# Seven channel tiles of the last FFN block convolved by TensorE, with second products, row maxima and scaling laid out anew in the slot before it

## The chip, the core and the metric

The kernel runs on one core of a Trainium2 chip: TensorE (PE), VectorE (DVE), ScalarE (ACT), GpSimd (POOL), and SyncE (SP), which issues the DMAs. The metric is the device time of one execution in microseconds, lower is better.

## The reference, cut to what matters

The input x is 4 batches x 2048 rows x 512. A cross attention adds to it first; then comes the FFN, of which the change touches the last block of rows:

```python
h = bit_linear(x, w1)                     # act_quant: each row scaled by 127 / its largest |value|, rounded
h = depthwise_conv1d(h.transpose(0, 2, 1), conv_w, conv_b)   # 2048 channels, 3 taps along the rows, padding 1
h = jax.nn.silu(h.transpose(0, 2, 1))
return bit_linear(h, w2)                  # the same quantisation, now over the row's 2048 channels
```

bit_linear uses weights rounded to -1, 0 and 1. Its row maximum makes the second product wait until all 2048 channels of a row are there. The outputs of this layer are x plus attention, plus the FFN of the layer norm of that.

## The kernel before, in words

The 8192 rows go in 16 blocks of 512 (NB = 16), the FFN's 2048 channels in 16 tiles of 128 (CT = 16). Each engine runs its own list of instructions in the order in which the code is written, and semaphores tie the lists together. The work is staged in slots. In slot s the kernel projects the queries of block s + 1, does the attention of block s, the first product, convolution and silu of block s - 1, and the second product of block s - 2. Slot NB - 1 = 15 is the last with attention; slot NB = 16 has only the FFN middle of the last block and the second product of the one before; slot 17 is the last block's second product, whose result is stored as the program's end.

The FFN middle of one channel tile c goes through five steps. TensorE forms the first product (`mm1`, L864) in one of two PSUM banks. `dequant` on VectorE (L1591) scales it into g, a ring of four buffers, so that tile c waits until tile c - 4 is convolved. `neighbours` on ScalarE (L1164) copies the two edge columns, `tap0` (L1262) forms the first tap, `taps` on VectorE (L1666) adds the middle one. The third tap is GpSimd's (L642 multiplies, L644 adds) for the tiles in `TAP.pool`, otherwise VectorE's (L1670). Then ScalarE does the silu (L1267). In slot 16 GpSimd has ten tiles of the third tap, VectorE six.

After the middle, VectorE takes the maxima over all channels (L1675, in the last block L1684), TensorE turns them (`turn_pm`, L1020), VectorE forms the scales (`scales2`), TensorE spreads them over the partitions (`spread_scales`, L1026), and ScalarE copies them to r2. Then h is multiplied by r2 (`scaled`: L654 on GpSimd, L1756 on VectorE), ScalarE rounds it to hqb (`rounded`, L1164), and `mm2` (L1042, in slot 17 L1144) is the second product. `result` (L1790) adds it to the rows. Slot 16 also computes again the outputs of the 12 rows at the ends of the blocks (the functions whose names begin with fix), on a few partitions or columns.

In slot 15 the attention's output is turned (`turn_o`, L946) and projected (`project_out`, L956); `residual` (L1736), `centre` (L1324), `square` (L1329) and `quantise` lead to the rounded rows (L1439), which TensorE turns (`turn_xq`, L1003) for the first product of slot 16.

## Time and profile before

| | before |
|---|---|
| median of 3 runs | 1532.26 us (1530.31 to 1534.05) |
| the profiled execution's own time | 1529.84 us |
| its span, first to last instruction | 1528.0 us |
| busy in the span | PE 95%, DVE 85%, ACT 77%, POOL 68% |
| mean granted TensorE clock | 0.977 |

The shares are means over 18 slots. The change touches only what runs after about 1394 us; there PE is busy 67% of the stretch from 1437 to 1487 us, and VectorE 86%. All the times below are in us from the first instruction. The granted clock is 1.00 for 2.4 GHz and 0.50 for 1.2 GHz.

### The profile page before, as it was taken

The numbers are of one execution on the slowest core, as the hardware profiler recorded it, in microseconds if no ns is written. First come the engines' busy times: TensorE is split into PE (matmuls) and PEld (weight loads), VectorE is DVE, ScalarE is ACT, GpSimd is POOL, SyncE is SP. The second block draws the span as 40 slices with busy tenths as digits, with TensorE's granted clock in tenths as the row PEclk, the third lists the DMA queues.
The fourth block names the chain that finished last, engine by engine and source line by source line (L and its number), as shares of the span: only waits on it lengthen the run. The fifth ranks groups of instructions, "written<-read, shape, count | busy, mean of one in ns | idle before, by whom it ended". The sixth has DMA issues, their size and how long they took to land.

```text
span 1528.0 us, 24767 instructions
## 1 busy us (share of the span) xinstructions
PE 1446.3 (95%) x9060; PEld 886.2 (58%) x9060; DVE 1298.4 (85%) x2014; ACT 1184.1 (77%) x2176; POOL 1035.2 (68%) x838
## 2 busy tenths in 40 slices
PE   9998988999999999999999999999999999998866
PEld 6474745657575656656575656656574756555322
DVE  7787796897979898898979898898989898978796
ACT  3567788979687888879687878889687878887652
POOL 4011567868676968869676869778776869777552
PEclk9998999999999999999999999999999999998987
DMA  8551002030211203031202103031202101020000
GB/s 260 147 189 42 29 8 70 8 102 18 68 42 27 79 8 98 8 102 22 78 29 50 55 9 96 8 102 29 87 12 63 43 23 54 8 71 1 31 29 28
DMA packets 80343, 85.20 MB, mean 56 GB/s; under 512 B 29983, under 2 KB 55839, under 8 KB 79709
## 3 DMA queue, kind: packets, MB, share of 16 engines
q1 hardware_dynamic: 80221, 83.62, 18.9%
q8 instruction: 71, 1.16, 0.3%
q14 instruction: 51, 0.42, 0.1%
HBM read 38.74 MB, written 19.42 MB: 38 GB/s over the span
## 4 chain that ended last, share of the span: by engine, by line
PE 67%; DVE 19%; ACT 9%; issue 3%; POOL 2%; DMA 0%; SPq 0%; DVEq 0%; ACTq 0%
PE ps L858 13%; PE ps L683 12%; DVE negm L1750 11%; PE ps L956 10%; PE ps L864 10%; PE ps L1042 8%; ACT hqb L1164 4%; ACT pexp L1243 3%; PE ps L827 3%; DVE h L1666 2%; PE ps L946 2%; PE ps L924 1%; PE ps L1026 1%; POOL h L644 1%; PE ps L1012 1%
## 5 line engine op out<-in xcount | busy, mean ns | idle before, releaser
L644 POOL TENSOR_TENSOR h<-h,gall 128x512 f32<-128x512 f32 x235 | 347.9, 1480 | 18.4
L654 POOL TENSOR_TENSOR h<-h,r 128x512 f32<-128x512 f32 x240 | 306.7, 1324 | 58.9 <-ACT r L1164 58.9
L642 POOL TENSOR_TENSOR gall<-gall,cw 128x512 f32<-128x512 f32 x235 | 257.5, 1096 | 111.0 <-DVE h L1666 111.0
L1666 DVE SCALAR_TENSOR_TENSOR h<-gall,cw,h 128x512 f32<-128x512 f32 x256 | 261.9, 1026 | 49.5 <-ACT h L1262 49.3
L858 PEld LDWEIGHTS ps<-va,pexp 128*128 128x128 f32 x2048 | 259.5, 192 | 29.0 <-issue 10.9
L1591 DVE SCALAR_TENSOR_TENSOR gall<-ps,bias,srow 128x512 f32<-128x512 f32 x256 | 191.3, 747 | 86.7 <-POOL h L644 57.7
L864 PE MATMUL ps<-xqT,w1T 128*128 128x512 f16 x1024 | 258.0, 382 | 7.1 <-DVE gall L1591 7.1
L858 PE MATMUL ps<-va,pexp 128*128 128x33 f32 x2048 | 257.7, 270 | 0.0
L1042 PE MATMUL ps<-w2T,hqb 128*128 128x512 fp8e4 x960 | 240.2, 379 | 0.0
L1262 ACT ACTIVATE h<-gall,cb,cw 128x512 f32<-128x512 f32 x256 | 222.2, 868 | 8.5
L1243 ACT ACTIVATE pexp<-ps 128x512 f32<-128x512 f32 x320 | 179.5, 588 | 54.5 <-PE ps L827 27.7
L1164 ACT ACTIVATE hqb<-h 128x512 f16<-128x512 f32 x276 | 173.9, 683 | 39.4 <-PE ps L1042 18.1
L1750 DVE TENSOR_REDUCE negm<-ps 128x4 f16<-128x616 f32 x256 | 185.7, 792 | 19.9 <-PE ps L975 14.8
L683 PE MATMUL ps<-hl,WqT 128*128 128x512 f16 x768 | 170.8, 379 | 2.7 <-DVE hl L1708 2.6
L1267 ACT ACTIVATE h<-h 128x512 f32<-128x512 f32 x256 | 155.4, 684 | 12.3 <-POOL h L644 11.7
L956 PE MATMUL ps<-WoT,pexp 128*128 128x512 f16 x512 | 156.0, 381 | 2.5 <-DVE xn L1729 2.5
L864 PEld LDWEIGHTS ps<-xqT,w1T 128*128 128x128 fp8e4 x1024 | 102.1, 112 | 85.9 <-DVE gall L1591 11.7
L1042 PEld LDWEIGHTS ps<-w2T,hqb 128*128 128x128 f16 x960 | 92.3, 98 | 80.9 <-issue 1.8
L658 POOL TENSOR_TENSOR nw<-nw,mhalf 128x4 f32<-128x4 f32 x16 | 16.3, 1017 | 175.7 <-DVE nw L1760 175.7
L683 PEld LDWEIGHTS ps<-hl,WqT 128*128 128x128 f16 x768 | 74.2, 98 | 91.5 <-issue 8.0
L975 PE MATMUL ps<-kB,hl 128*128 128x308 f16 x512 | 116.1, 305 | 10.9 <-DVE negm L1750 8.5
L1324 ACT ACTIVATE xn<-xr,sum 128x512 f32<-128x512 f32 x64 | 44.1, 717 | 80.9 <-DVE xr L1736 75.6
(222 smaller groups left out, 2312.0 us busy)
## 6 DMA issues: line engine op xcount, KB each, us to landing
qs<-hl SPq DMA_DIRECT2D x192, 128.0 KB, 2.4
xr<-in_x SPq DMA_DIRECT2D x16, 1024.0 KB, 5.4
out<-xr SPq DMA_DIRECT2D x64, 256.0 KB
h<-in_L_ffn_w SPq DMA_DIRECT2D x8, 1024.0 KB, 5.2
srow<-in_L_xattn_bo SPq DMA_DIRECT2D x15, 256.0 KB, 3.1
kst<-kh_scratch SPq DMA_DIRECT2D x32, 38.5 KB
xr<-in_ctx SPq DMA_DIRECT2D x1, 1024.0 KB
h<-in_L_xattn_Wk SPq DMA_DIRECT2D x1, 1024.0 KB, 8.0
```

The costliest lines, as they stand in the source:

```text
L642: gp.tensor_tensor(right, right, cw[:, c, 2:3].to_broadcast([P, TB]), ALU.mult).then_inc(c2m_ok, 1)
L644: gp.tensor_tensor(hc(c), hc(c), right, ALU.add).then_inc(c2p_ok, 1)
L654: gp.tensor_tensor(hc(c), hc(c), r2[:], ALU.mult).then_inc(u_ok, 1)
L683: r = mm(bank, a, b_, start=i == 0, stop=i == n - 1, **kw)
L858: r = mm(o, pr[:, t * P:(t + 1) * P], rhs, start=j == 0 and t % 2 == 0, stop=j == J, skip_group_check=True)
L864: r = mm(F[(c + 1) % 2], w1T[:, k, c * P:(c + 1) * P], xqT[:, k, :], start=k == 0, stop=k == KT - 1)
L956: r = mm(bank, part(k)[:, i * P:(i + 1) * P], WoT[:, a, k, :], start=k == 0 and n == 0, stop=k == KT - 1 and n == 2)
L1042: r = mm(bank, hq(c)[:, i * P:(i + 1) * P], w2T[:, c, :], start=False, stop=c == CT - 1, skip_group_check=late_results(s))
L1164: return nc.scalar.activation(o, i, ACT.Copy, **kw)
L1243: nc.scalar.activation(pexp[:, i % 3, :], A[i % 2], ACT.Exp, scale=1.0 / QS).then_inc(e_ok, 1)
L1666: ve.scalar_tensor_tensor(out=hc(c), in0=g[:, c % 4, 1:TB + 1], scalar=cw[:, c, 1:2], in1=hc(c), op0=ALU.mult, op1=ALU.add).then_inc(c1_ok, 1)
L1750: ve.tensor_reduce(negm[:, i, k * J:(k + 1) * J].rearrange("p (b e) -> p b e", b=2), banks, AX.X, ALU.max, negate=True).then_inc(mx_ok, 1)
```

## The change

In slot 16 the odd channel tiles 1 to 13 (`CONV`) leave ScalarE's tap0, VectorE's taps and the third tap. TensorE convolves each by three f32 products of 512 columns with diagonal matrices of the tap weights, in PSUM banks A[2] and A[3], and ScalarE's silu reads PSUM and adds the bias. GpSimd keeps the third tap of eight tiles, VectorE that of tile 15. ScalarE makes the 21 diagonals of 128x128 in slot 15, in the space of the queries.

In slot 15 pieces of the second product (`mm2`) go ahead of and behind `turn_o`. VectorE's first two residuals go between the two maxima. All 16 tiles are scaled by GpSimd: ten in slot 15, six within slot 16, two behind each of the taps of tiles 0, 2 and 4. ScalarE rounds none of them before slot 16 and spreads the 16 roundings over its ten first steps by `NEXT`.

In slot 16 the second product of the block before moves to the end of the slot, with its four results; tile 0 to 7's maxima come ahead of the taps of tile 14. `fix_mm2` moves ahead of slot 17's products, and the small fix products use other banks.

```diff
@@ tables
+        CONV = (1, 3, 5, 7, 9, 11, 13)
+        def mid(s, c):
+            return at(s, CT, c + 1 - CT) - (sum(n <= c for n in CONV) if s == NB else 0)
-        TAP = Share((0, 1, 2, 3, 4, 5, 6, 8, 9, 10, 11, 12, 13, 14, 15), last=(0, 2, 3, 5, 6, 8, 9, 11, 12, 14))
-        SCALE = Share(tuple(range(CT)), last_but_one=(0, 1, 3, 4, 6, 7, 9, 10, 12, 14), last=(1, 4, 7, 10, 12, 14))
+        TAP = Share((0, 1, 2, 3, 4, 5, 6, 8, 9, 10, 11, 12, 13, 14, 15), elsewhere=CONV, last=(0, 2, 4, 6, 8, 10, 12, 14))
+        SCALE = Share(tuple(range(CT)), last_but_one=tuple(range(CT)), last=(1, 4, 7, 10, 12, 14))
-            return 8 if s < NB - 1 else 4
+            return 8 if s < NB - 1 else 0
+        NEXT = (0, 0, 2, 3, 4, 5, 7, 9, 11, 13, 16)
@@ GpSimd
+                    if s == NB and c in (0, 2, 4):
+                        scaled(range(10 + c, 12 + c))
...
-                    scaled(SCALE.pool(s))
+                    scaled(range(10) if s == NB - 1 else SCALE.pool(s))
@@ TensorE
+                def conv(c):
+                    n = CONV.index(c)
+                    if n == 0:
+                        pe.wait_ge(dg_ok, 3 * len(CONV))
+                    if n >= 2:
+                        pe.wait_ge(si_ok, at(s, CT, CONV[n - 2] + 1 - CT))
+                    pe.wait_ge(g_ok, at(s, CT, c + 1 - CT))
+                    for k in (1, 2, 0):
+                        if k == 0:
+                            pe.wait_ge(nb_ok, at(s, CT, c + 1 - CT))
+                        r = mm(conv_bank(c), dg[:, n, k, :], g[:, c % 4, k:TB + k], start=k == 1, stop=k == 0)
+                    r.then_inc(cv_ok, 1)
...
+                    if c >= 2 and on_pe(s, c - 2):
+                        conv(c - 2)
...
-                    if s == NB and c in (8, 10, 12, 14):
-                        mm2((c - 8) // 2)
+                    if s == NB and c in (14, 15):
+                        mm2(0, range(CT // 2 * (c % 2), CT // 2 * (c % 2 + 1)))
...
+                        if s == NB - 1:
+                            mm2(0, range(0, 11))
                         turn_o()
+                        if s == NB - 1:
+                            mm2(0, range(11, CT))
+                            mm2(1, range(0, 4))
...
                 if s == NB:
+                    mm2(1)
                     fix_turn_pm()
+                    mm2(2, range(0, 8))
                     fix_scales()
+                    mm2(2, range(8, CT))
+                    mm2(3, range(0, 8))
                 if do_f:
                     turn_pm()
-                if do_a and do_m:
+                if s == NB:
+                    mm2(3, range(8, CT))
@@ ScalarE
+                def diagonal(n, k):
+                    nc.scalar.activation(dg[:, n, k, :], identf[:], ACT.Copy, scale=cw[:, CONV[n], k:k + 1]).then_inc(dg_ok, 1)
+                def silu_conv(c):
+                    act.wait_ge(cv_ok, CONV.index(c) + 1)
+                    nc.scalar.activation(hc(c), conv_bank(c), ACT.Silu, bias=cb[:, c:c + 1]).then_inc(si_ok, 1)
@@ VectorE
-                    if s == NB and c in (10, 12, 14, 16):
-                        result((c - 10) // 2)
-                    if s == NB and c == 14:
+                    if s == NB and c == 13:
                         fix_conv()
+                    if s == NB and c == 16:
+                        absmax_last(0, 4, pm)
+                        fix_absmax()
...
-                    for c in SCALE.dve(s)[:3]:
-                        scaled(c)
                     result(2)
-                    for c in SCALE.dve(s)[3:]:
-                        scaled(c)
                     result(3)
                 if s == NB:
                     fix_scaled()
+                    for i in range(1, TT):
+                        result(i)
                     for c in SCALE.dve(s):
                         scaled(c)
```

The first place is GpSimd's list from the end of slot 15 on. L654 is the scaling (it writes h with the factors r2), L642 and L644 are the third tap, L637 is the inverse root of the fix rows. Before:

```order
L654 TENSOR_TENSOR h<-h,r 128x512 [waits r2c,ln2]
L654 TENSOR_TENSOR h<-h,r 128x512 x9
L642 TENSOR_TENSOR gall<-gall,cw 128x512 [waits c1_ok]
L644 TENSOR_TENSOR h<-h,gall 128x512 [waits c2m_ok]
L642 TENSOR_TENSOR gall<-gall,cw 128x512 [waits c1_ok]
L644 TENSOR_TENSOR h<-h,gall 128x512 [waits c2m_ok]
L642 TENSOR_TENSOR gall<-gall,cw 128x512 [waits c1_ok]
L644 TENSOR_TENSOR h<-h,gall 128x512 [waits c2m_ok]
L637 TENSOR_TENSOR xn<-xn,mhalf 36x1 [waits fx_dve]
L642 TENSOR_TENSOR gall<-gall,cw 128x512 [waits c1_ok]
```

And now, where L660, L673, L675 and L668 are the same four:

```order
L660 TENSOR_TENSOR h<-h,r 128x512 [waits r2c,ln2]
L660 TENSOR_TENSOR h<-h,r 128x512 x9
L673 TENSOR_TENSOR gall<-gall,cw 128x512 [waits c1_ok]
L675 TENSOR_TENSOR h<-h,gall 128x512 [waits c2m_ok]
L660 TENSOR_TENSOR h<-h,r 128x512 x2
L673 TENSOR_TENSOR gall<-gall,cw 128x512 [waits c1_ok]
L675 TENSOR_TENSOR h<-h,gall 128x512 [waits c2m_ok]
L660 TENSOR_TENSOR h<-h,r 128x512 x2
L668 TENSOR_TENSOR xn<-xn,mhalf 36x1 [waits fx_dve]
L673 TENSOR_TENSOR gall<-gall,cw 128x512 [waits c1_ok]
L675 TENSOR_TENSOR h<-h,gall 128x512 [waits c2m_ok]
L660 TENSOR_TENSOR h<-h,r 128x512 x2
```

Two scalings stand behind each of the first three taps, so the tap of tile 2 and the inverse root come later in the list.

The second place is ScalarE's list in the second half of slot 15, from the centring of the attention's rows (L1324) to the rounded rows (L1439). Before:

```order
L1324 ACTIVATE xn<-xr,sum 128x512 [waits x2_ok] x2
L1324 ACTIVATE xn<-xr,sum 128x512 [waits op_ok,x2_ok]
L1324 ACTIVATE xn<-xr,sum 128x512 [waits x2_ok]
L1329 ACTIVATE osb,sq<-xn 128x512 [waits zx_ok] x4
L1164 ACTIVATE r<-ps 128x512 [waits r2_ok]
L1439 ACTIVATE osb<-xr,qb,qm 128x512 [waits ln2]
L1439 ACTIVATE osb<-xr,qb,qm 128x512 x3
L1164 ACTIVATE xqT<-ps 128x512 [waits xqt_ok] x4
```

And now (L1326 makes diagonals, L1400 centres, L1405 squares, L1524 rounds):

```order
L1326 ACTIVATE qs<-identf,cw 128x128 x6
L1400 ACTIVATE xn<-xr,sum 128x512 [waits x2_ok] x2
L1326 ACTIVATE qs<-identf,cw 128x128 x6
L1400 ACTIVATE xn<-xr,sum 128x512 [waits op_ok,x2_ok]
L1326 ACTIVATE qs<-identf,cw 128x128 x3
L1400 ACTIVATE xn<-xr,sum 128x512 [waits x2_ok]
L1405 ACTIVATE osb,sq<-xn 128x512 [waits zx_ok] x4
L1326 ACTIVATE qs<-identf,cw 128x128 x6
L1224 ACTIVATE r<-ps 128x512 [waits r2_ok]
L1524 ACTIVATE osb<-xr,qb,qm 128x512 [waits ln2]
L1524 ACTIVATE osb<-xr,qb,qm 128x512 x3
L1224 ACTIVATE xqT<-ps 128x512 [waits xqt_ok] x4
```

Nine diagonals stand between the second and the fourth centring, six between the squares and the copy of the factors.

The third place is TensorE's list in slot 16 from the first product of tile 8 (L864) on. Before:

```order
L864 MATMUL ps<-xqT,w1T 128x512 [waits g_ok]
L864 MATMUL ps<-xqT,w1T 128x512 x3
L864 MATMUL ps<-xqT,w1T 128x512 [waits g_ok]
L864 MATMUL ps<-xqT,w1T 128x512 x3
L1040 MATMUL ps<-csum,negh 128x512 [waits hq_ok]
L1042 MATMUL ps<-w2T,hqb 128x512 x16
L864 MATMUL ps<-xqT,w1T 128x512 [waits g_ok]
L864 MATMUL ps<-xqT,w1T 128x512 x3
L887 MATMUL ps<-identh,osb 128x36 [waits fx_act]
L887 MATMUL ps<-identh,osb 128x36 x3
L889 MATMUL ps<-identf,xn 128x36
L864 MATMUL ps<-xqT,w1T 128x512 [waits g_ok]
L864 MATMUL ps<-xqT,w1T 128x512 x3
```

And now (L893 is the first product, L907 the convolution by diagonals, L930 and L932 are fix_turn, L938 is fix_mm1):

```order
L893 MATMUL ps<-xqT,w1T 128x512 [waits g_ok]
L893 MATMUL ps<-xqT,w1T 128x512 x3
L893 MATMUL ps<-xqT,w1T 128x512 [waits g_ok]
L893 MATMUL ps<-xqT,w1T 128x512 x3
L907 MATMUL ps<-gall,qs 128x512 [waits g_ok,si_ok]
L907 MATMUL ps<-gall,qs 128x512
L907 MATMUL ps<-gall,qs 128x512 [waits nb_ok]
L930 MATMUL ps<-identh,osb 128x36 [waits fx_act]
L930 MATMUL ps<-identh,osb 128x36 x3
L932 MATMUL ps<-identf,xn 128x36
L893 MATMUL ps<-xqT,w1T 128x512 [waits g_ok]
```

The second products (L1042) are gone from here, and three f32 products stand behind the first product of each odd tile.

## Rows read from the trace of the kernel before

**Rows 1.** Windows by stage: span of the stretch, busy us of each engine, PE clock

```profile
1437.07:1486.73 49.66, 33.45 (x195) 13.51 (x194) 42.87 (x61) 33.78 (x66) 30.62 (x25) 0.89 0.08 29
1486.73:1498.25 11.52, 0.97 (x3) 0.58 (x3) 11.30 (x12) 1.22 (x2) 1.23 (x1) 0.50 0.00 0
```

**Rows 2.** Timeline, slot 15: start, length, engine, line, idle before and its releaser

```profile
1415.04 1.95 ACT L1324 ACTIVATE xn<-xr,sum 128x512 f32<-128x512 f32 x3 [5.82 <-DVE xr L1736]
...
1417.46 0.72 ACT L1324 ACTIVATE xn<-xr,sum 128x512 f32<-128x512 f32 x1 [0.48 <-DVE xr L1736]
...
1420.67 0.17 DVE L1760 TENSOR_SCALAR nw<-sq 128x4 f32<-128x4 f32 x1
...
1423.57 0.17 DVE L1783 TENSOR_SCALAR qb<-qb 128x4 f32<-128x4 f32 x1
...
1425.68 0.60 ACT L1164 ACTIVATE r<-ps 128x512 f32<-128x512 f32 x1 [5.05 <-PE ps L1026]
...
1429.60 0.90 PEld L1003 LDWEIGHTS ps<-identh,osb 128*128 128x128 f16 x16 [0.58 <-ACT osb L1439]
```

**Rows 3.** Groups by shape, ScalarE, whole run: count, busy us, mean ns

```profile
L1164 ACT ACTIVATE gall<-gall 128x2 f32<-128x2 f32 x256 | 51.7, 202 | 6.6 <-DVE gall L1591 6.2
L1164 ACT ACTIVATE xn<-xn 128x192 f16<-128x192 f32 x1 | 0.4, 363 | 11.9 <-DVE xn L1657 11.9
```

**Rows 4.** Timeline, from slot 15 to 16

```profile
1436.40 4.63 ACT L1164 ACTIVATE hqb<-h 128x512 f16<-128x512 f32 x8 [3.58 <-PE ps L1042]
...
1437.07 1.40 DVE L1591 SCALAR_TENSOR_TENSOR gall<-ps,bias,srow 128x512 f32<-128x512 f32 x2
...
1442.87 1.04 POOL L642 TENSOR_TENSOR gall<-gall,cw 128x512 f32<-128x512 f32 x1 [1.19 <-DVE h L1666]
```

**Rows 5.** GpSimd's groups: three in 1436 to 1487 us, the scaling in the whole run

```profile
L644 POOL TENSOR_TENSOR h<-h,gall 128x512 f32<-128x512 f32 x10 | 15.6, 1558 | 0.8
L642 POOL TENSOR_TENSOR gall<-gall,cw 128x512 f32<-128x512 f32 x10 | 10.8, 1082 | 18.3 <-DVE h L1666 18.3
L637 POOL TENSOR_TENSOR xn<-xn,mhalf 36x1 f32<-36x1 f32 x1 | 1.0, 1001 | 0.0
...
L654 POOL TENSOR_TENSOR h<-h,r 128x512 f32<-128x512 f32 x240 | 306.7, 1324 | 58.9 <-ACT r L1164 58.9
```

**Rows 6.** Timeline, TensorE: f32 products at both clocks, first products at both

```profile
1430.51 1.11 PE L1012 MATMUL ps<-identf,qm 128*128 128x128 f32 x8
...
1444.49 1.80 PE L864 MATMUL ps<-xqT,w1T 128*128 128x512 f16 x4 [3.70 <-DVE gall L1591]
...
1451.61 1.04 PE L864 MATMUL ps<-xqT,w1T 128*128 128x512 f16 x4 [0.67 <-DVE gall L1591]
...
1500.89 2.08 PE L1026 MATMUL ps<-identf,qm 128*128 128x128 f32 x8 [1.52 <-DVE qm L1704]
```

**Rows 7.** VectorE, slot 16: two groups of 1436 to 1487 us, then its timeline

```profile
L1666 DVE SCALAR_TENSOR_TENSOR h<-gall,cw,h 128x512 f32<-128x512 f32 x16 | 14.2, 893 | 2.3 <-ACT h L1262 2.3
...
L1670 DVE SCALAR_TENSOR_TENSOR h<-gall,cw,h 128x512 f32<-128x512 f32 x6 | 8.8, 1473 | 0.2
...
1454.46 0.15 DVE L1604 TENSOR_TENSOR xn<-xn 36x1 f32<-36x1 f32 x1 [0.45 <-POOL xn L637]
...
1456.68 0.14 DVE L1621 TENSOR_SCALAR xn<-xn 36x1 f32<-36x1 f32 x1
...
1474.20 0.81 DVE L1628 TENSOR_TENSOR xn<-ps,bias 128x288 f32<-128x288 f32 x2
...
1478.33 0.36 DVE L1638 TENSOR_TENSOR xn<-xn,cb 128x192 f32<-128x192 f32 x1
```

**Rows 8.** Timeline, from the end of slot 16 to the last products

```profile
1503.68 10.32 POOL L654 TENSOR_TENSOR h<-h,r 128x512 f32<-128x512 f32 x6 [15.72 <-ACT r L1164]
...
1509.22 13.99 PE L1144 MATMUL ps<-w2T,hqb 128*128 128x512 fp8e4 x64
...
1514.59 4.02 ACT L1164 ACTIVATE hqb<-h 128x512 f16<-128x512 f32 x7 [1.03 <-DVE h L1756]
```

More of the change, by code:

```diff
@@ L374, in dve @@
             def dve(self, s):
-                return tuple(c for c in range(CT) if c not in self.pool(s))
+                return tuple(c for c in range(CT) if c not in self.pool(s) and not (s == NB and c in self.elsewhere))
             def done(self, s, c):
@@ L630, in slot, with scaled @@
                 do_q, do_a, do_f, do_m = stages(s)
+                def scaled(tiles):
+                    for c in tiles:
+                        gp.tensor_tensor(hc(c), hc(c), r2[:], ALU.mult).then_inc(u_ok, 1)
                 for c in range(CT):
@@ L1372, in slot @@
                     if do_m and s != NB + 1:
-                        for k in range(early(s - 1) + 2 * c, min(early(s - 1) + 2 * c + 2, CT)):
+                        for k in late_roundings(s, c):
                             rounded_late(k)
@@ L1838, in slot @@
                         norm1()
-                    if do_f and c >= 2:
+                    if do_f and c >= 2 and not on_pe(s, c - 2):
                         taps(c - 2)
@@ L1878, in slot @@
                     centred_max(1)
+                if s == NB:
+                    result(0)
                 if do_f:
```

94 lines of the change are left out of this document (65 added, 29 removed).

## The prediction

> **What bounds the kernel now.** I read the windows by stage first, then the chain that ended last, then the timeline from 1379 us on, with the two instruction lists beside it. Up to slot 15 both lists are the same, so the first 1394 us can't change. Behind them no engine is full. From 1437 to 1487 us, the FFN middle of the last block, TensorE is busy 33 of 50 us, GpSimd 31, ScalarE 34, VectorE 43 [rows 1]. There each of VectorE's instructions waits for another engine's turn, or shares its time with GpSimd's: the middle tap has a mean of 0.89 us, the third tap 1.47 [rows 7]. Then come 11.5 us of maxima on VectorE, with TensorE idle at clock 0.50 [rows 1], and at the end the last scalings, roundings and 64 products, which run to 1523.2 us [rows 8]. So what counts is how early each of four handovers comes: the rounded rows in slot 15, the first dequantised tile, the last tile's maxima, the first scaling by r2.
>
> **The change, step by step.**
>
> *Slot 15, to the turned rows.* TensorE's pieces of the second product go where it waits anyway, and the row factors no longer stand behind two whole second products: the copy of r2 waited 5.05 us for TensorE [rows 2]. What is late next is ScalarE. A diagonal has 128 columns, between the 2 columns at 0.20 us and the 192 at 0.36 [rows 3]; by the line between them 0.30 us. Six of the 21 go where ScalarE waited 5.82 us for the first residual [rows 2]. The two residuals between the maxima leave VectorE's sum alone, so the second residual still ends at about 1415. From there: centring 0.65, six diagonals 1.8, centring 0.65, three diagonals 0.9, centring 0.7, to 1419.7 instead of 1418.2 [rows 2]. The squares end 1.5 us later, at 1422.1 instead of 1420.67, and the quantising scalars, which take 3.1 us to 1423.7 [rows 2], end at 1425.2. The last six diagonals and the copy of r2 run meanwhile. The rounded rows took 3.3 us from 1426.3 on, so TensorE can turn them at 1428.5, not 1429.6 [rows 2]: 1.1 us won.
>
> *Into slot 16.* Before, eight products of the last second product ahead of the first product, eight more behind it, and six scalings on VectorE put the first dequantisation at 1437.07, and eight roundings of 4.63 us kept ScalarE from tile 0 until 1441 [rows 4]. Now five products of 0.22 us [rows 8] follow the turned rows (1.1 us) and the spread row (1.0), the first product ends at 1432.5, and the dequantisation starts at 1432.6; ScalarE has two roundings and is at tile 0 by 1433.4. VectorE's tap of tile 0 is there at 1436. But GpSimd isn't: its ten scalings begin at 1425.2 with the scalars and take 10 x 1.32 [rows 5], to 1438.4. It was 1442.87 [rows 4]: 4.5 us won of some 7.5.
>
> *GpSimd, then the fix rows.* GpSimd is now the late one. It goes on with the tap of tile 0 (1.08 + 1.56 [rows 5], 2.7 with the handover), two scalings, the tap of tile 2, two scalings and the inverse root of the fix rows (1.0): 5.4 + 5.3 + 1.0 puts the root at 1450.2. It ended at 1454.4 [rows 7], so this wait moves forward too, though its list has become longer by four scalings. The fix scalars stand ahead of the dequantisation of tile 7, and behind that are queued TensorE's first product of tile 9 and all behind it. They take 2.4 us [rows 7], the dequantisation 0.7 [rows 4]: 1453.3. The fix rows' loads from memory start behind the fourth result and so some 4.7 us earlier; they stay ahead of this.
>
> *TensorE in slot 16.* A convolution is three f32 products of 512 columns, and the trace has no such product. It has f32 products of 128 columns: four of them (recorded as eight) take 1.11 us at full clock with the drain of the last, 0.24 each from start to start, and 2.08 at half clock [rows 6]. Four times the columns give 0.86 to 0.96; the lower end is what the columns alone make of it, and I take it: 2.6 us for a tile, 18 us for seven. The most, at half clock throughout, is 5.2 a tile. From 1453.3 TensorE has first product 9, convolution 7, the fix turn, first products 10 and 11, convolution 9, the 64 small fix products and first product 12: 4 x 0.87 + 2 x 2.6 + 0.6 + 1.8 = 11.1 us. Before it TensorE has waited some 5 us; after waiting 3.7 us its clock was down and a first product took 1.80 instead of 1.04 [rows 6], so I add 1.8. First product 12 ends at 1466.2.
>
> The Trainium skill (Perfetto Trace Analysis, Engine Utilization) rates f32 in its low-high form at half of TensorE's peak; by it a 512-column product would be 0.43 us, an estimate, two convolutions of this list 2.6 us shorter and the forecast 2.6 us lower. FP8 and Floating Point Precision (TensorE Precision Notes) gives true f32 four passes, an estimate of 0.85 us. The row of 0.24 us for 128 columns sides with four passes.
>
> *VectorE to the last maximum.* From there VectorE is the path: dequantisation and tap 1.6, the small convolution of the fix rows 4.5 (1474.20 to 1478.7 [rows 7]), tiles 13, 14, 15 and the tap of 12 another 3.0, the maxima 11.5 [rows 1], and among them the taps of 14 and 15, 0.9 + 0.9 + 1.5 [rows 7]. That is 23.9 us, to 1490.1, against 1498.25: 8.1 us won. The seven tiles that VectorE and ScalarE no longer tap shorten lists that now wait for GpSimd and TensorE; in themselves they pay nothing more.
>
> *To the first scaling.* Two things are given back. TensorE has 17 products of 0.22 behind the fix scales, which come from VectorE 2.9 us ahead of its last maximum (one reduction of half length and a merge): 1487.2 + 0.4 + 3.7 = 1491.3, with 0.5 for a clock that may be down, 1491.8 for the turn. The turn and the spread are 1.5 us shorter at full clock [rows 6]; eight products of 1.75 lie between them over the 1.4 of scalars; and three results of 0.75 stand ahead of VectorE's first scaling. GpSimd starts at 1495.8, VectorE at 1496.5, instead of 1503.68 [rows 8]: 7.2 to 7.9 won.
>
> *The end.* The scalings and roundings keep their shape: 10.9 us from the first scaling to the last seven roundings [rows 8], so these start at about 1507.3. Their first is ready 0.6 later, and seven tiles of four products at 0.22 need 6.1: 1514.0. TensorE alone: spread at 1495.2, the fix product of 17 x 0.22 (now at full clock) and four preparing ones to 1499.8, then 13.99 [rows 8] to 1513.8. Both ends meet. It was 1523.2 with the drain of the last product, some 1522.6 without it. I take 8.5 us off. The profiled execution took 1529.84, so 1521.3; the median lies 2.4 us above it, which gives 1523.8. A measurement tells about 0.2% (3 us) from no change.
>
> **The rivals.**
>
> *GpSimd's price is the contended one.* I charge 1.32 us a scaling. When VectorE scaled at the same time it was 10.32 for six, 1.72 [rows 8]. Now VectorE mostly reads PSUM beside it in slot 15, but in slot 16 it taps. With 1.72 for the 14 scalings ahead of the root, 5.6 us are lost and 2.9 of the gain remain: 1529.4. For it speaks that GpSimd is now at the head of the chain; against it that the mean over 240 is 1.32 with VectorE busy beside it [rows 5]. GPSIMD Engine Reference (Key points) of the Trainium skill says that GpSimd contends with VectorE's instructions with two SBUF inputs; by this rule the four scalings in slot 16 pay and the ten in slot 15 mostly don't. 14 in 100.
>
> *Slower: the f32 products run at half clock.* All 35 us or so of first products and convolutions in slot 16 would double where the clock is 0.50. From 1453.3 to first product 15 TensorE has 17.5 us of work; at half clock throughout that is 15.7 us more than I allow, VectorE's list behind it has 1 us of slack, and the end moves by 14.5 to 6 us slower than before: 1538. It decides from about half of this stretch at the low clock on. The clock was 0.89 in this stretch with a less busy TensorE [rows 1], which speaks against it; what speaks for it is that each convolution waits for ScalarE and a silu. 8 in 100.
>
> *The gain is given back.* The late parts of slot 16 are a list of handovers I have priced at 0.05 to 0.1 us each. If the fix products, the scales and the second products block each other in TensorE's order by some 3 us twice, the outcome is within 3 us of before: 1531. 8 in 100.
>
> *More is won.* If TensorE's clock doesn't fall (1.8 and 0.5), the diagonals take 0.25, and the third taps lose their contention, as they have only one partner (0.3 x 4), 12 us are won: 1520 or a little lower. 8 in 100.
>
> My forecast has the rest, 62 in 100; its own range is a gain of 4.5 to 12 us.
>
> **How the numbers follow.** Faster: the forecast, more won, and two thirds of the contended case, 0.79. Same: the other third and most of the gain given back, 0.12. Slower: half clock and the rest, 0.09. The range runs from 1517.5, beyond the case of more won, to 1530, which takes in the contended case; half clock and part of the gain given back are left out.
>
> **What would show it.** Right: GpSimd without a gap from 1425 to the inverse root near 1450; three f32 products of 2.6 us in a tile's place; a TensorE gap of 5 us ahead of first product 9; maxima done near 1490; the last products near 1514. Wrong: ScalarE's diagonals much above 0.30, scalings of 1.5 and more, convolutions of 4 to 5 us, or results that hold VectorE's scalings beyond 1498.

## The result, and the profile after

The changed kernel takes 1521.57 us, the median of 4 runs (1519.37 to 1523.01), the kernel before 1532.49 (4 runs, 1530.31 to 1534.05): a ratio of 0.9934, with an interval of 0.9914 to 0.9953. 1523.8 was predicted, with a range of 1517.5 to 1530. The profiled execution took 1519.37 us with a span of 1517.6 and a mean granted clock of 0.988, against 1528.0 and 0.977. It was the shortest of the four.

Not all of the 10.4 us between the two spans comes from the change. The first of the view's rows below is GpSimd's inverse root in the first slot, the second the same root in slot 14, both far ahead of anything that was changed. In these rows the columns are start, length, engine, line, what is written from what, shapes, the number of instructions, and in brackets the idle time before it with what ended that. Before:

```profile
146.46 1.02 POOL L658 TENSOR_TENSOR nw<-nw,mhalf 128x4 f32<-128x4 f32 x1 [28.48 <-DVE nw L1760]
...
1339.33 1.02 POOL L658 TENSOR_TENSOR nw<-nw,mhalf 128x4 f32<-128x4 f32 x1 [9.82 <-DVE nw L1760]
```

After:

```profile
144.21 1.02 POOL L687 TENSOR_TENSOR nw<-nw,mhalf 128x4 f32<-128x4 f32 x1 [28.30 <-DVE nw L1847]
...
1337.15 1.02 POOL L687 TENSOR_TENSOR nw<-nw,mhalf 128x4 f32<-128x4 f32 x1 [9.79 <-DVE nw L1847]
```

2.25 us are there at the first root and 2.18 at slot 14's: the two executions differ in how long the preparation took, and in next to nothing from there to slot 14. Over all the kernels below, the first root lies between 144.21 and 148.56 us and slot 14's between 1337.15 and 1344.03, though the instructions ahead of them are the same. So I count from the root of slot 14 on; from there to the end it is 188.67 us before and 180.45 after, and the change itself has won **8.2 us**. The interval of the ratio is 7.2 to 13.2 us of gain, and 8.2 lies in it. In the table every time is counted so. It needs no more than subtraction: the row's start (or end) less the start of slot 14's root.

| from slot 14's root on, us | before | after | won | forecast |
|---|---|---|---|---|
| slot 16's first dequantisation | 97.74 | 93.19 | 4.6 | 4.5 |
| GpSimd's first tap | 103.54 | 98.74 | 4.8 | 4.5 |
| fix rows' inverse root, end | 115.10 | 109.96 | 5.1 | 4.2 |
| last maximum, end | 158.87 | 152.27 | 6.6 | 8.1 |
| VectorE's first scaling by r2 | 164.31 | 157.83 | 6.5 | 7.2 |
| last 64 products, start | 169.89 | 161.64 | 8.3 | |
| last instruction | 188.67 | 180.45 | 8.2 | 8.5 |

GpSimd from slot 15 on, in the changed kernel's timeline, where [rows 4, 5] stood before:

```profile
1422.89 13.03 POOL L660 TENSOR_TENSOR h<-h,r 128x512 f32<-128x512 f32 x10 [1.88 <-DVE qb L1870]
1435.89 1.04 POOL L673 TENSOR_TENSOR gall<-gall,cw 128x512 f32<-128x512 f32 x1
1437.01 1.30 POOL L675 TENSOR_TENSOR h<-h,gall 128x512 f32<-128x512 f32 x1
1438.26 3.01 POOL L660 TENSOR_TENSOR h<-h,r 128x512 f32<-128x512 f32 x2
...
1446.56 0.55 POOL L668 TENSOR_TENSOR xn<-xn,mhalf 36x1 f32<-36x1 f32 x1
...
1462.11 1.04 POOL L673 TENSOR_TENSOR gall<-gall,cw 128x512 f32<-128x512 f32 x1 [5.33 <-DVE h L1753]
```

It runs without a gap from 1422.89 to the inverse root at 1446.56, as forecast, at 1.30 us a scaling in slot 15 and 1.50 for the four ahead of the root in slot 16. From then on it waits, 5.33 us ahead of one tap: it was the late one only up to the root.

VectorE at the fix scalars, the tiles behind them, and the last maxima [rows 7 before]:

```profile
1447.15 0.99 DVE L1691 TENSOR_TENSOR xn<-xn 36x1 f32<-36x1 f32 x1 [1.70 <-POOL xn L668]
1448.17 0.15 DVE L1693 SCALAR_TENSOR_TENSOR xn<-xn 36x1 f32<-36x1 f32 x1
1448.36 1.14 DVE L1696 SCALAR_TENSOR_TENSOR xn<-xn 36x1 f32<-36x1 f32 x1
1449.54 1.48 DVE L1699 TENSOR_SCALAR osb<-osb,xn 36x512 f32<-36x512 f32 x1
...
1452.22 1.41 DVE L1678 SCALAR_TENSOR_TENSOR gall<-ps,bias,srow 128x512 f32<-128x512 f32 x2
...
1460.62 0.75 DVE L1678 SCALAR_TENSOR_TENSOR gall<-ps,bias,srow 128x512 f32<-128x512 f32 x1 [4.85 <-PE ps L893]
...
1488.73 0.69 DVE L1776 TENSOR_TENSOR pm<-pm,pexp 128x512 f32<-128x512 f32 x1
...
1491.40 0.69 DVE L1781 TENSOR_REDUCE qm<-ps 128x4 f32<-128x512 f32 x1 [1.32 <-PE ps L1063]
1494.98 12.54 DVE L1843 TENSOR_TENSOR h<-h,r 128x512 f32<-128x512 f32 x10
```

From the root to the next dequantisation it is 5.1 us (1447.15 to 1452.22). L1691 works on 36 numbers and takes 0.99; the row of this shape took 0.15 before [rows 7]. Beside these rows, GpSimd's of the same time are to be laid, still of the changed kernel:

```profile
1447.09 1.03 POOL L673 TENSOR_TENSOR gall<-gall,cw 128x512 f32<-128x512 f32 x1
1448.20 1.29 POOL L675 TENSOR_TENSOR h<-h,gall 128x512 f32<-128x512 f32 x1
1449.44 2.71 POOL L660 TENSOR_TENSOR h<-h,r 128x512 f32<-128x512 f32 x2
```

VectorE's L1691 ends at 1448.14, GpSimd's L673 at 1448.12. L1693 starts at 1448.17, in the 0.08 us between two of GpSimd's instructions, and takes 0.15. L1696 ends at 1449.50, GpSimd's L675 at 1449.49. L1699 ends at 1451.02, GpSimd's first scaling of this pair at 1450.73. The kernel before shows the same instructions with GpSimd waiting beside them for 3.83 us, and L1699's pass over 36x512 (there L1612) takes 0.54, not 1.48:

```profile
1455.02 0.54 DVE L1612 TENSOR_SCALAR osb<-osb,xn 36x512 f32<-36x512 f32 x1
...
1458.26 1.04 POOL L642 TENSOR_TENSOR gall<-gall,cw 128x512 f32<-128x512 f32 x1 [3.83 <-DVE h L1666]
```

TensorE in the same stretch, with the three f32 products as L907, and the end [rows 6, 8 before]:

```profile
1432.88 2.74 PE L907 MATMUL ps<-gall,qs 128*128 128x512 f32 x6
...
1453.03 1.89 PE L893 MATMUL ps<-xqT,w1T 128*128 128x512 f16 x4 [7.50 <-DVE gall L1678]
1454.70 4.41 PE L907 MATMUL ps<-gall,qs 128*128 128x512 f32 x6
...
1486.56 0.39 PE L948 MATMUL ps<-identf,xn 12*128 12x12 f32 x2 [1.74 <-DVE xn L1740]
1486.88 1.90 PE L1087 MATMUL ps<-w2T,hqb 128*128 128x512 fp8e4 x8
...
1490.76 0.60 PE L1063 MATMUL ps<-identf,pm 128*128 128x128 f32 x4
...
1498.79 14.18 PE L1206 MATMUL ps<-w2T,hqb 128*128 128x512 fp8e4 x64
```

A convolution (three products, recorded as six) takes 2.74 us at full clock, counted to the end of its last product, which still runs while the next instruction has started. The one behind the wait of 7.50 us takes 4.41. Its granted clock stands in the windows (length, busy us of PE, PEld, DVE, ACT and POOL, clock):

```profile
1430.34:1482.67 52.33, 44.31 (x208) 19.02 (x206) 35.56 (x47) 27.94 (x58) 33.21 (x28) 0.90 0.03 8
1482.67:1489.42 6.75, 5.01 (x22) 2.01 (x23) 6.58 (x11) 1.23 (x2) 1.23 (x1) 1.00 0.00 0
...
1449.00:1450.00 1.00, 0.00 (x0) 0.00 (x0) 0.96 (x2) 0.00 (x0) 1.00 (x2) 0.50 0.00 0
...
1456.00:1458.00 2.00, 2.00 (x3) 0.67 (x2) 0.00 (x0) 1.97 (x4) 0.79 (x1) 0.50 0.00 0
1458.00:1459.00 1.00, 1.00 (x3) 0.19 (x1) 0.00 (x0) 0.04 (x1) 0.00 (x0) 0.97 0.00 0
```

The clock fell during the wait, and was back at 1458. Where the maxima ran at 0.50 before [rows 1], TensorE now has second products beside them and stays at 1.00. Over the FFN middle, TensorE is busy 44 of 52 us and VectorE only 36. From 1453.03 on TensorE's list is what VectorE waits for (4.85 us once, in the rows above): until 1484.8 TensorE itself waits only once, for 0.47 us.

### The profile page after: what moved, and what is told of

The parts are those of the page before. It is cut to its first block and busy times, and to the rows that moved or that the text cites. A ratio compares the mean times of both kernels' runs of the same rounds, so it can differ in the third digit from the quotient of the medians.

```text
span 1517.6 us, 24856 instructions
## 1 busy us (share of the span) xinstructions
PE 1456.6 (96%) x9102; PEld 890.7 (59%) x9102; DVE 1270.8 (84%) x1996; ACT 1185.8 (78%) x2190; POOL 1035.4 (68%) x840
## 5 line engine op out<-in xcount | busy, mean ns | idle before, releaser
L675 POOL TENSOR_TENSOR h<-h,gall 128x512 f32<-128x512 f32 x233 | 344.9, 1480 | 18.2
L660 POOL TENSOR_TENSOR h<-h,r 128x512 f32<-128x512 f32 x246 | 313.1, 1318 | 50.9 <-ACT r L1224 49.0
L673 POOL TENSOR_TENSOR gall<-gall,cw 128x512 f32<-128x512 f32 x233 | 255.3, 1096 | 109.8 <-DVE h L1753 109.8
L1753 DVE SCALAR_TENSOR_TENSOR h<-gall,cw,h 128x512 f32<-128x512 f32 x249 | 253.4, 1020 | 46.9 <-ACT h L1322 46.7
L887 PEld LDWEIGHTS ps<-va,pexp 128*128 128x128 f32 x2048 | 259.5, 192 | 29.0 <-issue 10.9
L893 PE MATMUL ps<-xqT,w1T 128*128 128x512 f16 x1024 | 256.1, 380 | 8.1 <-DVE gall L1678 8.0
L1322 ACT ACTIVATE h<-gall,cb,cw 128x512 f32<-128x512 f32 x249 | 216.4, 869 | 8.3
L1341 ACT ACTIVATE h<-h 128x512 f32<-128x512 f32 x249 | 151.0, 684 | 13.8 <-POOL h L675 13.4
L893 PEld LDWEIGHTS ps<-xqT,w1T 128*128 128x128 fp8e4 x1024 | 101.8, 111 | 86.1 <-DVE gall L1678 11.8
L1400 ACT ACTIVATE xn<-xr,sum 128x512 f32<-128x512 f32 x64 | 44.3, 717 | 77.8 <-DVE xr L1823 71.4
```

What stands on the lines that cost most here:

```text
L660: gp.tensor_tensor(hc(c), hc(c), r2[:], ALU.mult).then_inc(u_ok, 1)
L673: gp.tensor_tensor(right, right, cw[:, c, 2:3].to_broadcast([P, TB]), ALU.mult).then_inc(c2m_ok, 1)
L675: gp.tensor_tensor(hc(c), hc(c), right, ALU.add).then_inc(c2p_ok, 1)
L887: r = mm(o, pr[:, t * P:(t + 1) * P], rhs, start=j == 0 and t % 2 == 0, stop=j == J, skip_group_check=True)
L893: r = mm(F[(c + 1) % 2], w1T[:, k, c * P:(c + 1) * P], xqT[:, k, :], start=k == 0, stop=k == KT - 1)
L1322: nc.scalar.activation(hc(c), g[:, c % 4, 0:TB], ACT.Identity, bias=cb[:, c:c + 1], scale=cw[:, c, 0:1]).then_inc(c0_ok, 1)
```

## The experiments

Each was timed beside the kernel before on its chip. Repeated runs of one kernel lie 1 to 7 us apart, and in the profiles much of that lies ahead of slot 14's root, so the reading goes by the profile from that root on. "End" is that time: 188.67 before, 180.45 after. The first four go out from the changed kernel.

Each kernel has one profile, so two things are to be kept in mind. Where kernels have the same lists up to a point, their times from the root on agree closely: slot 16's first dequantisation stands at 91.74 to 91.78 us in e4, e6, e9 and e10. But TensorE's clock can fall in one execution ahead of the turn of the maxima and not in another, and this alone moves the end by 1.6 us (below, under e6). Differences under 2 us at the end are therefore read at the last maximum too. The timed ratios are too coarse for them: e4's is no better than the changed kernel's, and e5's no better than e2's.

| | timed ratio | end | root | last maximum | first VectorE scaling |
|---|---|---|---|---|---|
| before | | 188.67 | 115.10 | 158.87 | 164.31 |
| after | 0.9934 | 180.45 | 109.96 | 152.27 | 157.83 |
| e1, no convolution on TensorE | 0.9990 (0.9980 to 0.9999) | 188.12 | 112.54 | 157.13 | 165.49 |
| e2, slot 15 of before | 0.9935 (0.9918 to 0.9952) | 178.63 | 110.44 | 150.44 | 156.00 |
| e3, root early | 0.9919 (0.9899 to 0.9938) | 177.28 | 101.67 | 147.47 | 154.62 |
| e4, diagonals early | 0.9941 (0.9923 to 0.9959) | 179.40 | 108.54 | 151.19 | 156.75 |
| e5, e2 with root early | 0.9941 (0.9918 to 0.9963) | 178.02 | 106.45 | 148.25 | 155.40 |
| e6, e3 and e4 | 0.9910 (0.9891 to 0.9930) | 174.23 | 100.21 | 146.02 | 151.57 |
| e7, e6, VectorE scales too | 0.9917 (0.9893 to 0.9941) | 175.25 | 103.18 | 145.46 | 152.61 |
| e8, e5, eight products moved up | 0.9948 (0.9932 to 0.9964) | 181.44 | 106.45 | 150.38 | 158.86 |
| e9, e6, fix rows a step earlier | 0.9907 (0.9890 to 0.9923) | 174.17 | 100.24 | 144.39 | 151.54 |
| e10, e6, six tiles on TensorE | 0.9924 (0.9911 to 0.9938) | 177.58 | 100.25 | 147.07 | 154.98 |

**e1: without the convolution.** The seven tiles get their taps from ScalarE, VectorE and GpSimd again, and there are no diagonals; all else is as in the changed kernel.

```diff
-        CONV = (1, 3, 5, 7, 9, 11, 13)
-        TAP = Share(..., elsewhere=CONV, last=(0, 2, 4, 6, 8, 10, 12, 14))
+        CONV = ()
+        TAP = Share(..., elsewhere=CONV, last=(0, 2, 3, 5, 6, 8, 9, 11, 12, 14))
```

> The changed kernel without its convolution on TensorE: CONV is empty, all tiles go through the three taps, GpSimd has the third tap of the ten tiles of before. Everything else stays. The change as a whole won 10.9 us in the medians and 8.3 us in the two traces from slot 14's inverse root to the end. Theory: the convolution is what makes the room, since GpSimd is at the head of slot 16 and has six scalings more; without it VectorE has 42 us of work in slot 16 again, with waits some 46, and the maxima end 6 to 9 us later than in the changed kernel, so that 0 to 3 us of the gain over before are left. Rival: the gain comes from slot 15 and from taking the second products out of slot 16's middle; then the time stays within 2 us of the changed kernel.

The end is at 188.12, 0.55 us ahead of before. So 7.7 of the 8.2 us need the convolution on TensorE; everything else that was moved is worth 0.55 without it. The maxima come 1.7 us earlier than before, but the first scaling 1.2 us later: VectorE then waits 4.11 us for the turn, behind TensorE's second products, sixteen of which take 3.59 and 2.57 us. Their clock had fallen in an earlier wait of 4.50 us: it stands at 1.00 from 1483 to 1485 us of this trace and at 0.50 from 1486 to 1498. At the last maximum the convolution is worth 4.9 us (157.13 against 152.27). The reverse, the convolution without any of the rearrangement, was not run; e2 comes nearest to it.

**e2: slot 15 of before.** The pieces of the second product, the residuals, the scalings (six on VectorE) and the early roundings stand where they stood before, and GpSimd has no scalings in slot 16. The diagonals stay where the change put them, nine of them between the centrings.

```diff
-        SCALE = Share(tuple(range(CT)), last_but_one=tuple(range(CT)), last=(1, 4, 7, 10, 12, 14))
+        SCALE = Share(tuple(range(CT)), last_but_one=(0, 1, 3, 4, 6, 7, 9, 10, 12, 14), last=(1, 4, 7, 10, 12, 14))
-                        if s == NB - 1:
-                            mm2(0, range(0, 11))
...
-                        if s == NB - 1:
-                            mm2(0, range(11, CT))
-                            mm2(1, range(0, 4))
```

> The changed kernel with slot 15 as before (second products, residuals, six scalings on VectorE, four roundings at its end, no scalings in slot 16), the diagonals stay. Theory, GpSimd at the head: its last scaling in slot 15 then ends at some 1441 us instead of 1436, but two taps later it is without the four scalings, so the inverse root of the fix rows comes within 1.5 us of where it does in the changed kernel, and the end with it: 0 to 2.5 us slower than the changed kernel. Rival, each handover is handed on: slot 16 starts 4.5 to 6 us later (first dequantisation some 7 us later) and the end is 4.5 to 6 us later.

It is 1.8 us faster, and I had expected it no faster. Slot 16 begins 4.9 us later, but the root ends only 0.5 later, since GpSimd has four scalings fewer ahead of it, and TensorE arrives later at the same wait. In e2's timeline it is 2.00 us long, and the clock stays up: the convolution behind it takes 2.74 us, not 4.41. From slot 14's root, TensorE goes on at 116.5 us here and at 115.9 in the changed kernel; the new slot 15 is 0.6 ahead there and then loses the 2.5 us of the low clock.

```profile
1455.09 1.04 PE L891 MATMUL ps<-xqT,w1T 128*128 128x512 f16 x4 [2.00 <-DVE gall L1669]
1455.96 2.74 PE L905 MATMUL ps<-gall,qs 128*128 128x512 f32 x6
```

**e3: the inverse root early.** It goes right behind the tap of tile 0, ahead of the four scalings and a tap, and the fix scalars one tile earlier.

```diff
-                    if s == NB and c == 4:
-                        pool.wait_ge(fx_dve, 3)
-                        gp.tensor_tensor(fnw[:, 1:2], fnw[:, 0:1], mhalf[0:N3, 0:1], ALU.pow).then_inc(fx_pw, 1)
+                    # the same three lines at c == 0, behind the tap of tile 0
-                    if s == NB and c == 7:
+                    if s == NB and c == 6:
                         fix_quantise()
```

> The changed kernel with GpSimd's inverse root of the fix rows right behind the tap of tile 0, ahead of all scalings of slot 16, and the fix rows' scalars on VectorE ahead of tile 6 instead of tile 7, where VectorE waited 2.9 us. Theory: the wait for this root held TensorE 7.5 us and let its clock fall; without it the dequantisation of tile 7 comes at 1446 to 1447 us of the changed kernel's trace instead of 1452.2, the convolution of tile 7 takes 2.7 instead of 4.4, and the end is 3 to 7 us earlier. Rival, GpSimd's load itself is the bound: the root was only one item, the taps of tiles 6 to 14 come at GpSimd's own pace and the end is at most 1.5 us earlier.

3.2 us faster: the wait at the root was what slot 16 lost. The maxima gain 4.8, the first scaling only 3.2. The missing 1.6 us are TensorE's second products ahead of the turn (L1063), most of them at half the clock in this execution:

```profile
1484.53 0.39 PE L948 MATMUL ps<-identf,xn 12*128 12x12 f32 x2 [1.75 <-DVE xn L1740]
1484.85 3.17 PE L1087 MATMUL ps<-w2T,hqb 128*128 128x512 fp8e4 x8
...
1488.49 2.00 PE L1087 MATMUL ps<-w2T,hqb 128*128 128x512 fp8e4 x8
1490.33 0.60 PE L1063 MATMUL ps<-identf,pm 128*128 128x128 f32 x4
```

The eight products behind L948, which took 1.90 us after a wait of 1.74 in the changed kernel, take 3.17 here after one of 1.75. The clock fell after TensorE had taken up work again: it is 1.00 from 1484.6 to 1485.2 and 0.50 from 1485.4 to 1488.6. VectorE's fix scalars still take 4.6 us here, at another place against GpSimd's list.

**e4: the diagonals early.** Nine diagonals go ahead of the second centring, where ScalarE waits, instead of between centrings.

```diff
+                    if s == NB - 1:
+                        diagonals(2, 5)
                     centre(1)
-                    if s == NB - 1:
-                        diagonals(2, 4)
                     centre(2)
-                    if s == NB - 1:
-                        diagonals(4, 5)
```

> The changed kernel with the nine diagonals that stood around the third centring moved ahead of the second centring, where ScalarE waited 3.3 us. Theory: they were on the path by 1.4 us, so squares, scalars and GpSimd's first scaling come 1.2 to 1.6 us earlier, and as GpSimd is at the head, the end too. Rival: VectorE's residuals or the second products set this handover, and the first scaling moves by under 0.4 us.

GpSimd's first scaling comes 1.4 us earlier, the end 1.05. The prediction's 1.5 us for the diagonals in the chain of centrings is measured with that.

**e5 and e6: the four corners.** e6 is e3 and e4 together. e5 is e2 with the early root, and with all fifteen diagonals that are due before the squares ahead of the first centring. In slot 15 of before these diagonals cost nothing: GpSimd's first scaling starts at 87.13 us in e2 and at 87.08 in e5.

> Slot 15 as before, and with it the two edits that helped singly: the root of the fix rows behind the tap of tile 0, and all 15 diagonals of the middle of slot 15 ahead of the first centring, where ScalarE waits 5.8 us. From slot 14's inverse root to the end the changed kernel takes 180.45 us, slot 15 as before alone 178.63. Theory: the late start of slot 16 (4.8 us) costs nothing because the wait for the root and TensorE's own list take it up; with the root early TensorE's list begins some 4 us after that of the root-early kernel, so the old slot 15 loses its advantage: 176.5 to 178.5. Rival: both edits add to it as they did alone (3.2 and 1.05): 174.4.

> The changed kernel with the root early and the nine diagonals ahead of the second centring. Alone they took 3.2 and 1.05 us off the 180.45 us from slot 14's inverse root to the end. Theory: GpSimd is at the head in both, so they add: 175.9 to 176.5. Rival: with the root early the end hangs on TensorE's second products (its clock fell before them, 3.17 us for eight), which the earlier start doesn't shorten: 177 and more.

| end (last maximum) | root late | root early | root and diagonals early |
|---|---|---|---|
| slot 15 of before | 178.63 (150.44) | | 178.02 (148.25) |
| new slot 15 | 180.45 (152.27) | 177.28 (147.47) | 174.23 (146.02) |

The new slot 15 costs 1.8 us while the root is late. With the root early it pays 0.7 (e3 against e5, whose diagonals are free), and with the diagonals early too 3.8 at the end, but 2.2 at the last maximum. The other 1.6 us of the 3.8 are the clock ahead of the turn, which fell in e5's execution and not in e6's. This settles e2's surprise: of the 4.9 us that the new slot 15 wins, the wait for the root left 0.6, and the clock that fell in it took more than these. e6 gains 6.2 us where the two parts add up to 4.2, and misses my interval on the good side. Here too 1.6 us are the clock: it fell in e3's execution.

For every kernel with seven or six tiles on TensorE, this is what stands ahead of the turn: how long TensorE waited for the fix scales, what the next eight second products took, and the time from the last maximum to VectorE's first scaling.

| | wait, us | eight products, us | maximum to scaling, us |
|---|---|---|---|
| after, e6 | 1.74 | 1.90 | 5.6 |
| e2, e4 | 1.75 | 1.90 | 5.6 |
| e3 | 1.75 | 3.17 | 7.2 |
| e5 | 1.75 | 2.87 | 7.2 |
| e7 | 1.74 | 2.60 | 7.2 |
| e9 | 2.01 | 2.55 | 7.2 |
| e8 | 3.48 | 3.59 | 8.5 |
| e10 | 4.11 | 3.59 | 7.9 |

The same wait of 1.74 to 1.75 us was followed by full clock in four kernels and by half the clock in three.

**e7: who scales.** e6 with the scalings shared in slot 15 as before: VectorE takes six, ScalarE rounds four early.

```diff
-        SCALE = Share(tuple(range(CT)), last_but_one=tuple(range(CT)), last=(1, 4, 7, 10, 12, 14))
+        SCALE = Share(tuple(range(CT)), last_but_one=(0, 1, 3, 4, 6, 7, 9, 10, 12, 14), last=(1, 4, 7, 10, 12, 14))
```

> The same, and only the scaling as before: ten tiles by GpSimd and six by VectorE in slot 15, four roundings at its end, none of it in slot 16's GpSimd list. The second products' places and the residuals between the maxima stay as in the change. Theory: it is this part of the old slot 15 that made it 1.8 us faster, by taking 8 us of scalings out of GpSimd's list in slot 16 and seven roundings out of ScalarE's way to the convolution of tile 7; the pieces of second products help by their own. From slot 14's root to the end 174 to 176. Rival: the six scalings on VectorE and their contention delay the first dequantisation by 2 to 4 us and cost what they save: 176.2 and more.

The first dequantisation comes 3.5 us later, and the end 1.0, inside the interval of the theory. But the last maximum comes 0.6 us earlier than in e6 (145.46 against 146.02); the end is late by the 1.6 us of the clock ahead of the turn. The timed ratios (0.9917 and 0.9910) don't part the two either, so which share is better isn't shown. What is shown is that with six scalings taken out of GpSimd's list in slot 16, a start that is 3.5 us late costs nothing at the last maximum.

This pair also shows what GpSimd's scalings cost VectorE. The fix scalars' pass over 36x512, first in e6, where two scalings run beside it, then in e7, where GpSimd has none in slot 16:

```profile
1445.79 1.49 DVE L1697 TENSOR_SCALAR osb<-osb,xn 36x512 f32<-36x512 f32 x1
...
1445.70 2.73 POOL L660 TENSOR_TENSOR h<-h,r 128x512 f32<-128x512 f32 x2
```

```profile
1446.80 0.54 DVE L1695 TENSOR_SCALAR osb<-osb,xn 36x512 f32<-36x512 f32 x1
```

From the first fix scalar to the next dequantisation it is 4.7 us in e6 and 3.7 in e7.

**e8: filling TensorE's gap.** In e5, half of the first second product goes ahead of the first product of tile 9, where I took TensorE to wait; the small fix product uses other banks.

```diff
-                    if s == NB and c in (14, 15):
-                        mm2(0, range(CT // 2 * (c % 2), CT // 2 * (c % 2 + 1)))
+                    if s == NB and c in (8, 14):
+                        mm2(0, range(0, 8) if c == 8 else range(8, CT))
```

> The first kernel of this set (slot 15 as before, root and diagonals early), with the first half of the first second product of slot 16 moved from behind tile 14's first product to behind tile 8's, where TensorE has a gap; the small fix product uses other banks. Theory: TensorE's list is on the path from tile 9 on and its last second products stand ahead of the turn of the maxima, so 2 us of products taken out of it come off the end: 1.5 to 2 us less than the kernel without it. Rival: VectorE's list (small convolution, taps, maxima) is the bound there, and the end moves under 0.5 us, or the piece delays the convolution of tile 7.

3.4 us slower, against an expected gain. My error is plain in e5's timeline: with the root early, TensorE goes from tile 8 to tile 9 without a gap; and the second half had moved up too, so nothing left the list ahead of the last tile. The maxima come 2.1 us later, about the 2.1 us that the products take; TensorE then waits 3.48 us for the fix scales, and the next eight products take 3.59:

```profile
1485.18 0.60 PE L946 MATMUL ps<-identf,xn 12*128 12x12 f32 x2 [3.48 <-DVE xn L1729]
1485.71 3.59 PE L1087 MATMUL ps<-w2T,hqb 128*128 128x512 fp8e4 x8
```

**e9: the fix rows one step earlier.** From e6, so that the small convolution stands ahead of tile 12; ScalarE's two steps of this chain move with it.

```diff
-                    if s == NB and c == 9:
+                    if s == NB and c == 8:
                         fix_turn()
-                    if s == NB and c == 11:
+                    if s == NB and c == 10:
                         fix_mm1()
-                    if s == NB and c == 13:
+                    if s == NB and c == 12:
                         fix_conv()
```

> The changed kernel with root and diagonals early, and the fix rows' whole chain one step earlier: ScalarE's quantising copy and its two copies, TensorE's turn and 64 small products, and VectorE's small convolution ahead of the dequantisation of tile 12 instead of tile 13. From slot 14's inverse root to the end the kernel without this takes 174.23 us. Theory: VectorE waits 3.3 us for TensorE ahead of tile 12 while the small convolution of 4.7 us stands on its path behind it; moved into the wait it comes off by 2 to 3.5 us at the maxima, of which TensorE's second products ahead of the turn leave 1 to 2: 172.2 to 173.3. Rival: the earlier small products only push TensorE's first products of tiles 11 and 12 back and the copies hold ScalarE, the end is within 0.5 us or later.

The maxima come 1.6 us earlier, a little short of the 2 to 3.5 I expected, and the end not at all. TensorE's sixteen second products ahead of the turn take it: they wait for nothing of the last maxima, and ran at a low clock after a wait of 2.01 us. In e6 the same products ran at full clock, which is worth just these 1.6 us.

```profile
1485.56 0.39 PE L948 MATMUL ps<-identf,xn 12*128 12x12 f32 x2 [2.01 <-DVE xn L1738]
1485.88 2.55 PE L1087 MATMUL ps<-w2T,hqb 128*128 128x512 fp8e4 x8
1488.36 0.60 PE L1085 MATMUL ps<-csum,negh 1*128 1x512 f16 x1
1488.90 2.62 PE L1087 MATMUL ps<-w2T,hqb 128*128 128x512 fp8e4 x8
1491.36 0.60 PE L1063 MATMUL ps<-identf,pm 128*128 128x128 f32 x4
```

**e10: six tiles.** From e6, tile 13 goes back to the taps.

```diff
-        CONV = (1, 3, 5, 7, 9, 11, 13)
+        CONV = (1, 3, 5, 7, 9, 11)
```

> The kernel with root and diagonals early, with six tiles convolved by TensorE instead of seven: tile 13 goes back to the three taps, its third on GpSimd. It takes 2.6 us out of TensorE's list and puts 0.9 us into VectorE's, 0.9 into ScalarE's and 2.5 into GpSimd's. Theory: VectorE's list from tile 12 to the maxima is on the path to the end, with GpSimd's last taps in it, while TensorE's second products follow close: the maxima come 0.5 to 1.5 us later, the end is 0 to 1 us later (174.2 to 175.2 us from slot 14's root). Rival: TensorE is the bound from tile 9 on, and 2.6 us out of its list take 1 to 2.5 us off the end.

3.35 us slower, where I had expected 1 at most. Of that 1.05 are at the maxima; the rest is a wait of 4.11 us for the fix scales and the clock behind it (3.59 and 2.12 us for two times eight products). With less work TensorE came to the fix scales sooner, waited longer for them, and its clock fell in the wait.

The best are e6 and e9, which can't be told apart: 1516.22 us (ratio 0.9910) and 1516.61 (0.9907), each beside its own runs of the kernel before. The changed kernel stands at 0.9934; the timed intervals overlap, and what says that e6 is faster is the profile: 6.2 us from slot 14's root on, and 6.25 at the last maximum.

## Why the prediction was right, and where its terms were off

**What carries the gain.** The prediction had the seven tiles "pay nothing more" in themselves and put the gain on earlier handovers. The end fits, but this reading does not: e1 keeps all the rearrangement and loses nearly all of the gain. The lists that the convolution shortens are what lets the handovers move; the seven tiles carry most of the gain. The forecast's sum was right because it counted VectorE's list without those taps (23.9 us from tile 12 to the last maximum); the sentence about it was wrong.

**Slot 15 and the start of slot 16.** Six diagonals in 1.85 us are 0.31 each, against 0.30; the turned rows start at 1426.27, 1428.45 in the time of before, against 1428.5; the first dequantisation at 1430.34, so 1432.5 against 1432.6; the first tap 1438.07 against 1438.4. e4 confirms the 1.5 us in its chain. That GpSimd was the late one up to the root is shown by e3 and e4.

**The fix scalars: the term that was mis-sized.** 2.4 us were taken from the rows of before, and they took 5.1. Before, GpSimd waited behind its inverse root; now it goes straight on with a tap and two scalings, and three of VectorE's instructions beside them take 0.99, 1.14 and 1.48 us instead of 0.15, 0.15 and 0.54. The first two end with GpSimd's, however short they are by themselves. In e3 and e6 the chain starts elsewhere against GpSimd's list, and L1691's counterpart takes 0.55 us in both; it ends again with GpSimd's instruction (in e6 at 1444.38, GpSimd's at 1444.37). In e1 it starts just behind the first of two scalings, and the instruction on 36 numbers takes 2.48 us:

```profile
1451.65 2.48 DVE L1691 TENSOR_TENSOR xn<-xn 36x1 f32<-36x1 f32 x1 [2.80 <-POOL xn L668]
...
1451.60 2.52 POOL L660 TENSOR_TENSOR h<-h,r 128x512 f32<-128x512 f32 x2
```

SBUF — State Buffer (SBUF: two separate sides) of the Trainium skill says that GpSimd and a VectorE instruction with two SBUF inputs, or in a two-port mode, lock each other out for whole instructions; the pairs of ends agree with it to 0.02 us. The late ones on 36x1 with one input (0.15 to 0.19 us) are not held up in the same stretch. For the scalings there is an experiment, e7 against e6: without them the pass over 36x512 takes 0.54 us again. For GpSimd's tap beside the first three scalars there is none, and its size is read from the traces.

**TensorE's wait and clock.** 5 us and a loss of 1.8 were forecast, 7.50 us and 2.5 came (1.89 instead of 1.04, 4.41 instead of 2.74). From the end of the root to TensorE's next product it is 5.9 us where 3.1 were allowed.

**How far the sum was luck.** Up to the last maximum four things went off, and they partly cancel: the root ended 0.9 us earlier than forecast (0.55 us long, not 1.0); the fix scalars and their handover cost 2.8 more; TensorE's list to the first product of tile 12 took 13.5 us instead of 12.9; VectorE's list from there took 22.9 instead of 23.9. That makes 6.6 us won instead of 8.1. From the last maximum to the end 1.6 us more were won, where the forecast had 0.4. So the end, 8.2 against 8.5, is closer than the terms behind it, and that closeness is luck. The median lies 2.2 us below the forecast for a reason that isn't in it: it moved by 10.9 us, of which the profiles give 8.2 to the change.

**The f32 product.** The three products repeat every 2.58 us at full clock, 0.86 each, the lower end, which the forecast took. FP8 and Floating Point Precision (TensorE Precision Notes) of the Trainium skill gives true f32 four passes, and the measurement agrees; the rule of Perfetto Trace Analysis (Engine Utilization), half of the peak, would make it an estimate of 0.43 and is not what this kernel shows.

**From the maxima to the end.** The turn came 1.34 us behind the last maximum, against 1.7, with TensorE's products in between at full clock; where the clock fell ahead of it, as in e3, e5, e7 and e9, it is 2.93. The scalings came at 1496.9 and 1497.2 in the time of before, against 1495.8 and 1496.5. The last products were TensorE's own affair: they start 8.3 us earlier, more than the scalings do, since the 16 small second products now run at full clock ahead of them (3.62 us). That returned 1.5 us, which the forecast had from the same term.

**The rivals.** The contended price of GpSimd is half true, where its condition said: 1.30 us a scaling in slot 15, 1.50 in slot 16, 0.7 us in all over the four ahead of the root. What the rival missed is that GpSimd's list costs VectorE more than VectorE's costs GpSimd: 2.8 us at the fix scalars. Half clock cost 2.5 us at one place, and the mean over the FFN middle is 0.90. Some gain was left lying at the root and in the diagonals, 6.2 us by e6, of which the forecast knew nothing.

What stays open: why the clock fell behind a wait of 1.74 to 1.75 us in e3, e5 and e7 and not in the changed kernel, e2, e4 and e6. With one profile a kernel, no run says whether it belongs to the kernel or to the execution.

## What to carry to other kernels

When an engine's idle time is given to new work, look at what stands behind that work on the same queue for somebody else: one instruction of 0.55 us, queued behind four scalings, decided whether the rearrangement of a whole slot cost 1.8 us or paid 0.7. An experiment that undoes one of two coupled parts tells little by itself; the corners of both told it. What is put beside a chain of small instructions on the neighbouring engine can cost it more than its own length suggests. And where executions scatter by more than the effect, count from the last place where both programs are the same.

## What the runs showed of the hardware

- VectorE and GpSimd hold each other up down to the smallest instruction: one on 36x1 took 0.55, 0.99, 1.15 and, beside two scalings, 2.48 us, where it takes 0.15 alone; one that started in a gap of 0.08 us between two of GpSimd's kept its 0.15. A pass over 36x512 took 1.48 instead of 0.54.
- Leaving TensorE idle costs later, not at the wait. After 7.50 us the clock was at 0.50 for another five us of work; after 4.11 and 3.48 us eight products took 3.59 instead of 1.90; after 1.74 to 1.75 us they took 1.90 in four kernels and 2.60 to 3.17 in three. In e3 the clock fell 0.8 us after TensorE had taken up work again.
- Taking work off TensorE can therefore lengthen the program: with six tiles instead of seven the end came 3.35 us later, 1.05 of them at the last maximum and the rest behind a longer wait of TensorE.
- The same instructions up to slot 14 took 1337.15 us in one execution and 1344.03 in another; on one chip (e2 and e4) 1338.57 and 1342.70.
